# A Fourier network tower on TensorE: a looped instruction stream, and the last inverse transform on 64x64 tiles

## The reference

```
x = coords @ fc0_w + fc0_b                      # 64 images of 64x64, 3 -> 32 channels
for each of 4 layers:
    x_ft = rfft2(x)[:, :, :20, :20]             # 20 x 20 modes
    out  = einsum('bixy,ioxy->boxy', x_ft, w)   # complex mix of the channels, per mode
    x1   = irfft2(out padded with zeros)
    x2   = einsum('bchw,oc->bohw', x, cw) + cb  # 1x1 convolution
    x    = gelu(x1 + x2)
h = fc2(gelu(fc1(x)))                           # 32 -> 64 -> 1
h = h + attention(layernorm(h)); h = h + experts(layernorm(h))
```

## Time and profile before

| | us |
|---|---|
| median of three runs | 1643.8 |
| the runs | 1635.84, 1643.80, 1652.51 |
| span of the profiled execution, first to last instruction | 1633.9 |
| steady rounds of layers 0, 1, 2 (one pair each) | about 95 to 355, 410 to 680, 730 to 1005 |
| layer 3 | 1036 to 1229 |
| head | 1229 to 1371 |
| attention and experts | 1371 to 1634 |

### The profile page before, as it was taken

How to read it: one execution, slowest core, us unless ns; L and a number is a source line. 1 busy time by engine, 2 the same in 40 slices (tenths; PEclk the granted TensorE clock), 3 DMA queues, 4 the chain that set the end, 5 groups by cost and what they waited for, 6 DMA issues and landing times. The chain is left out here.

```text
span 1633.9 us, 44034 instructions
## 1 busy us (share of the span) xinstructions
PE 1550.8 (95%) x19928; PEld 896.7 (55%) x19928; DVE 1190.1 (73%) x1433; ACT 603.2 (37%) x929; POOL 92.3 (6%) x45
## 2 busy tenths in 40 slices
PE   9899999998999999999999999899999999989996
PEld 3555555555555555565555555777772115963332
DVE  3598899886989989878998998655540115887886
ACT  2433232223332232232322322444449996330221
POOL 1000000000000000000000000000000000007551
PEclk9999999999999999999999999999999999899998
DMA  6333332235655566556556556499998782037430
GB/s 218 114 125 130 128 133 104 120 125 214 247 231 233 207 225 237 215 177 256 214 214 237 222 209 231 139 362 356 354 354 330 255 287 72 1 73 186 110 85 13
DMA packets 59962, 316.30 MB, mean 194 GB/s; under 512 B 16576, under 2 KB 18688, under 8 KB 25984
## 3 DMA queue, kind: packets, MB, share of 16 engines
q1 hardware_dynamic: 36512, 177.99, 32.5%
q10 hardware_dynamic: 23264, 135.49, 20.2%
HBM read 176.09 MB, written 137.36 MB: 192 GB/s over the span
## 5 line engine op out<-in xcount | busy, mean ns | idle before, releaser
L835 ACT ACTIVATE act_c<-slots,conv_b 128x512 f32<-128x512 f32 x512 | 352.6, 689 | 734.0 <-PE slots L550 734.0
L550 PEld LDWEIGHTS slots<-inv_w,inv_out 128*128 128x128 f32 x4096 | 499.4, 196 | 188.2 <-issue 178.9
L550 PE MATMUL slots<-inv_w,inv_out 128*128 128x128 f32 x4096 | 541.8, 287 | 4.8 <-DVE inv_out L725 4.8
L725 DVE STREAM_TRANSPOSE inv_out<-slots 128x1024 f32<-128x1024 f32 x256 | 303.9, 1225 | 98.1 <-PE slots L515 98.1
L701 DVE STREAM_TRANSPOSE turned_h<-slots 128x1024 f32<-128x1024 f32 x200 | 237.9, 1228 | 27.5 <-PE slots L448 26.5
L690 DVE STREAM_TRANSPOSE turned_w<-act_c 128x1024 f32<-128x1024 f32 x192 | 224.9, 1208 | 1.1 <-ACT act_c L835 1.1
L448 PE MATMUL slots<-turned_w,fwd_w 32*64 32x512 f32 x3200 | 200.0, 607 | 3.0 <-DVE turned_h L701 2.5
L707 DVE STREAM_TRANSPOSE modes<-slots 128x640 f32<-128x640 f32 x96 | 81.0, 846 | 79.8 <-PE slots L460 79.8
L460 PE MATMUL slots<-turned_h,fwd_h 64*64 64x320 f32 x1600 | 136.4, 453 | 1.3 <-DVE turned_h L701 1.3
L537 PE MATMUL slots<-act_c,conv_w 32*32 32x512 f32 x3072 | 111.8, 604 | 19.3 <-DVE modes L707 15.4
L515 PE MATMUL slots<-turned_k,inv_h 32*64 32x320 f32 x2048 | 102.3, 455 | 8.3 <-DVE turned_k L715 6.9
(11 more groups left out here) (166 smaller groups left out, 1124.3 us busy)
## 6 DMA issues: line engine op xcount, KB each, us to landing
act_scratch<-act_c ACTq DMA_DIRECT2D x128, 1024.0 KB, 4.8
act_c<-act_scratch SPq DMA_DIRECT2D x128, 1024.0 KB, 5.2
mode_w<-in_sw_dram SPq DMA_DIRECT2D x20, 640.0 KB, 4.4
at_turned<-level_scratch SPq DMA_DIRECT2D x24, 256.0 KB, 4.2
at_ret_t<-level_scratch SPq DMA_DIRECT2D x20, 256.0 KB, 4.4
xin<-in_x_dram SPq DMA_DIRECT2D x4, 1024.0 KB, 8.1
turned_w<-in_x_turned_dram SPq DMA_DIRECT2D x3, 1024.0 KB, 5.9
at_straight<-level_scratch SPq DMA_DIRECT2D x10, 256.0 KB, 4.2
```

The source lines that it names most:

```text
L550: mm = nc.tensor.matmul(banks[:, p, at:at + 128], inv_out[:, t % 2, i, p, :, :, r].rearrange("p b o -> p (b o)"), inv_w[:, i, :], start=Fa ...
L725: nc.vector.transpose(dst, src).then_inc(inv_turned, 1)
L835: nc.scalar.activation(act_c[:, t % RING, :, p, :], banks[:, p, :].rearrange("p (i m) -> p i m", i=2), ACT.Gelu, bias=conv_b[:, l:l + 1]). ...
```

## The change

Four things change together.

- **`inverse_w` and `inverse_h` without the butterfly.** `inverse_h` computes all 64 rows at once, as 64x64 tiles (8 matmuls of 320 columns, as before 8). `inverse_w` becomes 64 matmuls a pair of 64x64 with 64 moving columns, on the four quarters of the array, in two calls of 32 (banks 0 and 1, banks 2 and 3). `inv_w` shrinks to 128 x 64.
- **A loop on PE.** The body of a pair is now `step(l, j)`. In layers 1 to 3 `steps` runs two pairs a round in a loop of PE's sequencer: pairs 4 to 29 of layers 1 and 2 (13 rounds each), pairs 1 to 30 of layer 3 (15 rounds). Layer 0 and the other pairs stay unrolled. Waits of a loop must name constants, so at the end of a round nops take from each semaphore what the round's waits used (`give_back`), and `take` counts on the host what has been taken.
- **Own buffers for the convolution's input.** SP loads into `xin`, two slots, from layer 1 on; `act_c` (four slots) only takes GELU's results. A load waits for the first half of `inverse_w` two pairs before. GELU waits for the store and the `dft_w` of the slot's last user.
- **GELU in two instructions of 1024** for four of 512, with a drain behind them, which releases `turn_act` and the store.

The diff, cut:

```diff
+IN_RING = 2
@@ dft_constants
-        for n in range(32):
-            outer, inner, r = n // 8, n // 2 % 4, n % 2
+        for p in range(4):
+            for n in range(32):
+                half, s, q, r = n // 16, n // 8 % 2, n // 2 % 4, n % 2
+                h = 32 * s + 8 * a + 2 * b + r
...
-        inv_h = sb("inv_h", [128, 2, 64])
-        inv_w = sb("inv_w", [128, 2, 128])
+        inv_h = sb("inv_h", [128, 2, 128])
+        inv_w = sb("inv_w", [128, WW])
@@ sync
             def load_act(l, t):
+                if t >= IN_RING:
+                    sp.wait_ge(summed, after_out(l, t - IN_RING, 0))
+                elif l > 1:
+                    sp.wait_ge(summed, after_out(l - 1, t + PAIRS - IN_RING, 0))
+                else:
+                    sp.wait_ge(summed, after_out(0, PAIRS - 1 - LIFT_E * (1 - t), 0))
+                sp.wait_ge(act_stored[t % RING], after_store(l - 1, t))
+                sp.dma_start(flat(xin[:, t % IN_RING]), act_dram[t]).then_inc(act_in[t % IN_RING], 16)
@@ tensor
+            taken = Counter()
+            def take(sem, value):
+                pe.wait_ge(sem, value - taken[sem.name])
+            def give_back(sem, count):
+                pe.nop().then_inc(sem, -count)
...
             def inverse_h(l, t):
                 for i in range(2):
-                    for kwh in range(2):
-                        for khh in range(2):
-                            b, half = 2 * kwh + khh, khh ^ i
-                            mm = nc.tensor.matmul(banks[half * 64:(half + 1) * 64, 4 + 2 * i + kwh, 0:320],
-                                                  inv_h[b * 32:(b + 1) * 32, l % 2, :],
-                                                  turned_k[b * 32:(b + 1) * 32, t % 2, i * 320:(i + 1) * 320],
+                    for s in range(2):
+                        for kwh in range(2):
+                            rows = slice(kwh * 64, (kwh + 1) * 64)
+                            mm = nc.tensor.matmul(banks[s * 64:(s + 1) * 64, 4 + 2 * i + kwh, 0:320],
+                                                  inv_h[rows, l % 2, s * 64:(s + 1) * 64],
+                                                  turned_k[rows, t % 2, i * 320:(i + 1) * 320],
                                                   start=True, stop=True)
...
+            def inverse_w(l, t, two):
                 for i in range(2):
                     for r in range(2):
-                        at = i * 256 + r * 128
-                        mm = nc.tensor.matmul(
-                            banks[:, p, at:at + 128],
-                            inv_out[:, t % 2, i, p, :, :, r].rearrange("p b o -> p (b o)"),
-                            inv_w[:, i, :], start=False, stop=True, skip_group_check=True)
+                        for s in range(2):
+                            for half in range(2):
+                                for odd in range(2):
+                                    rows, at = slice(odd * 64, (odd + 1) * 64), i * 256 + r * 128 + s * 64
+                                    mm = nc.tensor.matmul(
+                                        banks[half * 64:(half + 1) * 64, 2 * two + odd, at:at + 64],
+                                        inv_out[rows, t % 2, i, two, s, 2 * half:2 * half + 2, :, r].rearrange(
+                                            "p b o -> p (b o)"),
+                                        inv_w[rows, :], start=False, stop=True, skip_group_check=True)
                 mm.then_inc(summed, 1)
+            def step(l, j):
+                last = l == LAYERS - 1
+                if j + 1 < PAIRS:
+                    if j >= 3 and not last:
+                        take(w_turned, after_w_turned(forward(l + 1, j - 3), 1))
+                    else:
+                        take(inv_turned, after_inv_turned(l, j, 1))
+                    inverse_h(l, j + 1)
+                if j >= 4 and not last:
+                    take(modes_set, forward(l + 1, j - 4) + 1)
+                conv(l, j)
+                inverse_w(l, j, 0)
+                if j >= 2 and not last:
+                    take(act_turned, after_turn(l + 1, j - 2))
+                    if j + 1 < PAIRS:
+                        take(inv_turned, after_inv_turned(l, j + 1, 1))
+                    dft_w(forward(l + 1, j - 2))
+                inverse_w(l, j, 1)
+                if j >= 3 and not last:
+                    take(act_low, after_set(l, j))
+                    dft_h(forward(l + 1, j - 3), (l + 1) % 2)
+            def steps(l, first, count):
+                rounds = count // 2
+                used = [(act_high, 2), (inv_turned, 4), (modes_turned, 2), (act_in[0], 16), (act_in[1], 16)]
+                if l < LAYERS - 1:
+                    used += [(act_low, 2), (act_turned, 2), (w_turned, 4), (modes_set, 2)]
+                with pe.Fori(0, rounds):
+                    for j in range(first, first + 2):
+                        step(l, j)
+                    for sem, count in used:
+                        give_back(sem, count)
+                for sem, count in used:
+                    taken[sem.name] += count * rounds
...
+                first = 1 if last else 4
+                looped = 2 * ((PAIRS - 1 - first) // 2) if l > 0 else 0
+                for j in range(1, first):
+                    step(l, j)
+                if looped:
+                    steps(l, first, looped)
+                for j in range(first + looped, PAIRS):
+                    step(l, j)
@@ vector, turn_act
-                dve.wait_ge(act_set, after_out(f - 1, t, 3))
+                dve.wait_ge(act_ready, after_set(f - 1, t))
@@ scalar
-                    if l == 0 and t >= RING:
-                        act.wait_ge(act_turned, after_turn(1, t - RING))
-                        act.wait_ge(act_stored[t % RING], after_store(0, t - RING))
-                    for p in range(4):
-                        act.wait_ge(summed, after_out(l, t, p))
-                        nc.scalar.activation(act_c[:, t % RING, :, p, :], ..., ACT.Gelu).then_inc(act_set, 1)
-                    act.wait_ge(act_set, after_out(l, t, 3))
+                    if l > 0 or t >= RING:
+                        before = (l, t - RING) if t >= RING else (l - 1, t + PAIRS - RING)
+                        act.wait_ge(act_stored[t % RING], after_store(*before))
+                        if before[0] < LAYERS - 1:
+                            act.wait_ge(w_done, forward(before[0] + 1, before[1]) + 1)
+                    for two in range(2):
+                        at = slice(2 * two, 2 * two + 2)
+                        act.wait_ge(summed, after_out(l, t, two))
+                        nc.scalar.activation(act_c[:, t % RING, :, at, :], ..., ACT.Gelu).then_inc(
+                            act_high if two else act_low, 1)
+                    act.drain().then_inc(act_ready, 1)
```

More of the change, by code:

```diff
@@ L1 @@
+from collections import Counter
 from contextlib import ExitStack
@@ L90, in dft_constants @@
     places = 16 * (kwh ^ place % 2) + place
[L91 to L97, removed]
+    inv_w = np.zeros((2, 2, 32, WW))
+    inv_w[:, 0, places] = norm * cos.T
+    inv_w[:, 1, places] = -norm * sin.T
     f32 = np.float32
@@ L280, in tower @@
         mode_w_in = [sem(f"mode_w_in{s}") for s in range(RING_W)]
-        act_in = [sem(f"act_in{s}") for s in range(RING)]
+        act_in = [sem(f"act_in{s}") for s in range(IN_RING)]
+        head_in = [sem(f"head_in{s}") for s in range(RING)]
         act_stored = [sem(f"act_stored{s}") for s in range(RING)]
@@ L579, in _ @@
                         lift(q - 1, e)
-            pe.wait_ge(modes_set, QUARTERS)
+            take(modes_set, QUARTERS)
             for e in range(LIFT_E):
@@ L589, in _ @@
                 conv(l, 0)
-                pe.wait_ge(inv_turned, after_inv_turned(l, 0, 1))
+                take(inv_turned, after_inv_turned(l, 0, 1))
                 inverse_w(l, 0, 0)
                 inverse_h(l, 1)
-                for p in range(1, 4):
-                    inverse_w(l, 0, p)
-                for j in range(1, PAIRS):
-                    if j + 1 < PAIRS:
-                        if j >= 3 and not last:
-                            pe.wait_ge(w_turned, after_w_turned(forward(l + 1, j - 3), 1))
-                        else:
-                            pe.wait_ge(inv_turned, after_inv_turned(l, j, 1))
-                        inverse_h(l, j + 1)
-                    if j >= 4 and not last:
-                        pe.wait_ge(modes_set, forward(l + 1, j - 4) + 1)
-                    conv(l, j)
-                    for p in range(2):
-                        inverse_w(l, j, p)
-                    if j >= 2 and not last:
-                        pe.wait_ge(act_turned, after_turn(l + 1, j - 2))
-                        if j + 1 < PAIRS:
-                            pe.wait_ge(inv_turned, after_inv_turned(l, j + 1, 1))
-                        dft_w(forward(l + 1, j - 2))
-                    for p in range(2, 4):
```

(9 more changed lines are left out.)

119 lines of the change are left out of this document (61 added, 58 removed).

## The result

The changed kernel takes **1592.6 us** (median of four runs, 1591.2 to 1597.5) for 1639.8 of the kernel before (1628.1 to 1652.5): a ratio of **0.973**, 95% interval 0.969 to 0.977. Forecast were 1616 and a range from 1600. The gain is 47 us where I had 27, and the forecast stood on a median of the kernel before of 1643.8, 4 us above this one.

The account below looks back on a forecast made before the run. PE was taken as the bound, with DVE 10% behind in layers 0 to 2. Terms -19 (rounds of layers 0 to 2), -4 (layer 3), -4 (layer ends) sum to -27 us against 1643.8: 1616 us, range 1600 to 1682.

Parts of the forecast that it names:

- The mechanism: Whole kernel: PE is freed, DVE's chain then decides layers 0 to 2, DMA layer 3; total -27 us.
- the sum of DVE's chain: Layers 0 to 2, from one end of `turn_w` to the next, through `inverse_h` and DVE's transposes: 9.24 us a round.
- the term -19: Layers 0 to 2: rounds fall from 9.48 to 9.24 us, 81 x 0.24 = -19 us.
- Halves of `inverse_w`: `inverse_w` on small tiles: halves of some 1.1 us, 2.2 us in all for 4.16, pace going by columns.
- Layer 3: Layer 3's rounds: DMA decides, 5.8 us for 5.94 (bounds 5.64 and 5.94), -4 us (0 to -9).
- Ends of layers 0 to 2: Layer ends: longer `inverse_h` costs +1.1 us, last steps give back most of PE's 2; net -1 us a layer.
- Rival A: `inverse_w`: pace goes by the record, 30 ns, +37 us, 1680 us, slower; chance 0.15.
- Rival B: PE's loops: code is fetched anew after each branch, with layer 0 and the ends 1780 us, slower; chance 0.18.
- the stream for layer 0: Unrolled layer 0: 448 instructions are 1.8 packets, 7.8 us of a 9.24 us round, so code supply holds.
- The two input slots: Convolution input, two slots for four: costed at nothing; loads have 9.4 us in layer 3, median landing 7.6.
- GELU in two: GELU, 2.2 us for 2.8 a pair: hidden in a round; uncovered, 0.4 us a pair in layer 3.
- Nops and branch: End of a loop round: hidden by PE's idle time; without that cover 0.5 us x 41 = 20 us.

Follow-up runs that it names:

- `pad2`: Changed kernel plus two idle 128x128 matmuls (four records) on PE before `dft_h` in layers 0 to 2; 1604.5 us, ratio 0.980 to the kernel before.
- `dve_split`: Changed kernel with DVE's order changed: one of `turn_act`'s two transposes before `turn_w`, one behind it; 1577.8 us, ratio 0.964 to the kernel before.
- `half_load`: Changed kernel loading only one image of two in layer 3 from pair 2 on; 1579.4 us, ratio 0.966 to the kernel before.
- `body4`: Changed kernel with four pairs a round of the loop instead of two; 1649.7 us, ratio 1.009 to the kernel before.
- `butterfly`: Changed kernel with the old `inverse_h` and `inverse_w` tiles back; loop, input slots and two GELUs stay; 1661.5 us, ratio 1.016 to the kernel before.

## Why the prediction was wrong

**The mechanism stood.** PE got free, DVE's chain through banks 4 to 7 took over, with PE's two waits where I had put them (0.39 and 0.94 for 0.3 and 1.1), DMA took layer 3, the loop's code stayed on the chip. `pad2` in layer 0, `dve_split` and `half_load` show the first three by moving them, the packets the fourth.

**The step that failed is the sum of DVE's chain**, 9.24 us; it is 9.07, so the term -19 should have been -33. I had added start-to-start times of the trace before. One of them, `turn_act` to `turn_w`, 2.35, was not DVE's: L448 ends at 618.67, and `turn_w` starts at 618.78, 0.11 later, so it waited for PE. The hop is 0.11 in nearly every round before; in a layer's first two, where it is 0.17 and 0.30, the time is 2.27. In the changed kernel, with 0.78 between them, it is 2.24 to 2.26 (570.68 to 572.94). Where two transposes follow each other their records overlap by some 0.1; where the second starts just at the first one's recorded end, it was held. The second piece is `inverse_h`: I took hop, record and hop as 0.05 + 1.36 + 0.07, and it is 0.05 + 1.38 (575.35 to 576.73), for its record is 1.31. The 1.36 was `dft_h` behind matmuls of 128x128. Behind 64x64 tiles `dft_h` takes 1.31 too (573.10), without any idle time before it, and behind the 128x128 matmuls of `pad2` it takes 1.36 again. The two and 0.02 to 0.03 of `turn_w` make the 0.17 a round, on 81 rounds 14 us of the missing 20.

**How much that explains.** With the chain right the same sum gives 1602, just inside the range of 1600 to 1682. I had given bounds to layer 3 and to the ends, and none to the chain, the largest term. The rest of the way to 1592.6 is for the most part not the change: 4 us are the median of the kernel before, and 3.5 us, in the two profiled executions, the start and the last stage. These 7 or 8 us, which put the time below the range, are luck; that the sum was too small is not.

**The other terms.** Halves of `inverse_w`: priced at 1.1, measured 1.01 to the next start (572.09 to 573.10): 16 ns a record, 62 for four, where 59 had been scaled from the mixing by columns. The Trainium skill's 25 ns between starts ("TensorE: Matmul & The Clock Gate", the section on the clock gate) does not hold for these tiles; at 25 the 128 records would take 3.2 us and they take 2.15. Layer 3: 5.54 a round on average for 5.8, below the 5.64 that I took for DMA's least: the share rose to 0.99 and the rate to 377 GB/s, where 354 at 0.95 scale to 369. Its pairs give -6.7 after what the start takes back, with its end -5.3, for -4 and -1. Ends of layers 0 to 2, ramps with them: about -2.4 for -3. The start's +2.5 and the last stage's -6 are not the change's. -33.2 - 2.4 - 5.3 and these two give the -44.5 of the table, but for rounding.

**Rival A** (pace by the record) is refuted by 16 ns. **Rival B** is right as a mechanism and was wrong for this body: in `body4` the idle time at the branch is 4.33 us, 3.4 beyond the slack (I had +3.3), but two pairs are kept. The Trainium skill's rule ("Runtime: NRT & Kernel Launch", Instruction fetch mechanics), that a branch out of a two-page window waits for its fetch, doesn't hold for this body of 3.6 packets, while the branch of `body4`, 7.1 packets back, does wait; the room of 2048 instructions in the same section is too large for `body4`, whose 1800 were fetched anew. I had not asked what the tiles would cost without the loop: I priced the stream for layer 0 only, where it holds. In layer 3 it would have taken back the whole gain.

**Terms costed at nothing.** The two input slots: right as far as seen, DMA is full with them; another number was not tried. GELU in two: right while `inverse_h` covers it, 0.43 a round without (`butterfly`), as priced. Nops and branch: hidden in layers 1 to 3, and 0.3 to 0.8 a pass wherever the cover goes. What I had not thought of is the loop's first pass, whose code still has to come: the idle 3.65 us of layer 3 stand in it and end 2.4 us after a packet starts (1022.06). The drain, the two slots and the two GELUs were not tried each by itself.

**Open:** how much of the ends' slower clock and of `conv`'s wait in them could be saved, why the limit lies between 1400 and 1800 instructions, and what each of loop, buffers and GELU costs at the start of a layer (0.9 us in `butterfly`, whose first round is 5.42 for 4.48).

## What to carry to other kernels

A start-to-start time is only an engine's own if nothing held the later instruction: before adding such times to a chain that will decide, check the other engine's end beside each. When small tiles multiply the instructions, count packets of code per microsecond as well as columns: here one packet of 252 instructions came in 4.4 to 5.2 us, and layer 3, which needed them faster, had to loop over a body small enough to stay. And when a freed engine leaves another one waiting by turns, splitting one of the other's instructions into two places can cover the wait: 15 us here for a change of order.

## What was unexpected of the hardware

- Matmuls with 64 moving columns on four 64x64 tiles run at 16 ns a record, each with its own weight load (128 in 2.15 us).
- The code stream of an unrolled layer 3 gives one packet of 16 KB in 5.2 us, and a late packet is often paid twice, by 2.6 to 4 us of idle time and by a lower clock behind it (`inverse_h` 1.90 for 1.31).
- A loop of 1400 instructions on PE is fetched once, one of 1800 in every pass; a pass's branch with its nops costs 0.3 to 0.8 us when PE is the bound.
- The same 16 matmuls take 1.36 us behind 128x128 ones and 1.31 behind 64x64 tiles.
